# A four-layer graph network on one core: node rows lifted so that their mean carries the first norm's factor, and the first two node products joined

## The reference

```python
def _layernorm(x, axis=-1, eps=1e-05):
    m = jnp.mean(x, axis=axis, keepdims=True)
    v = jnp.var(x, axis=axis, keepdims=True)
    return (x - m) / jnp.sqrt(v + eps)
...
x = _layernorm(x + _L0_gnn_ref(x, edge_attr3_10x16, edge_index, ...))      # x + softplus MLP of summed edge rows
x = _layernorm(x + _L1_gnn_ref(x, edge_weight, src, dst, ...))             # (x W_self' + b + neighbours) / 2
x = _layernorm(x + _L2_gnn_ref(x, L2_gnn_w_s, L2_gnn_w_n, src, dst))       # relu(x w_s + neighbours)
x = _layernorm(x + _L3_gnn_ref(x, edge_index, ...))                        # two Chebyshev convolutions, hidden 256
return x
```

## Time and profile before

| | |
|---|---|
| three runs, median | 3864.7 us (3862.36 to 3864.95) |
| profiled execution | 3860.39 us, its span 3858.3 us |
| TensorE matmul busy | 3164.6 us, 82% of the span |
| VectorE busy | 3084.4 us, 80% |
| ScalarE busy | 2641.6 us, 68% |
| GpSimd busy | 2567.9 us, 67% |
| mean granted TensorE clock | 0.934 of 2.4 GHz |

### The profile page before, as it was taken

One profiled execution on the slowest core, in us unless ns is written; L12 is line 12 of the kernel. 1 busy time (PEld: TensorE's weight loads), 2 busy tenths in 40 slices (PEclk: granted clock), 3 DMA queues, 4 the chain that ended last, 5 costly groups with the idle time before them and its releaser, 6 DMA issues.

```text
span 3858.3 us, 74550 instructions
## 1 busy us (share of the span) xinstructions
PE 3164.6 (82%) x20774; PEld 2512.0 (65%) x20774; DVE 3084.4 (80%) x12882; ACT 2641.6 (68%) x7801; POOL 2567.9 (67%) x2650
## 2 busy tenths in 40 slices
PE   5779967777999999899999899989998999776100
PEld 2356656665888888678788766667777999665100
DVE  8979979997999999799899855557777888899200
ACT  0047769997888888699778777767766666698200
POOL 6757768884777777766477566645553666576676
PEclk9989979998999999999999999999999999988555
DMA  1056636564222222355455466657776777454432
GB/s 26 1 155 188 186 96 215 212 213 151 77 75 78 78 74 78 115 157 159 130 174 180 141 211 216 215 173 269 265 263 211 234 221 227 145 175 139 136 97 79
DMA packets 326132, 601.52 MB, mean 156 GB/s; under 512 B 71215, under 2 KB 99688, under 8 KB 325723
## 3 DMA queue, kind: packets, MB, share of 16 engines
q1 hardware_dynamic: 249434, 469.25, 36.3%
q0 software_dynamic: 76288, 127.51, 12.2%
HBM read 314.08 MB, written 283.99 MB: 155 GB/s over the span
## 4 chain that ended last, share of the span: by engine, by line
PE 47%; DVE 17%; POOL 15%; issue 9%; DMA 7%; ACT 4%; POOLq 1%; SPq 0%; DVEq 0%; ACTq 0%
PE ps L1670 7%; PE ps L1581 7%; PE ps L1528 6%; PE ps L1648 6%; PE ps L1727 4%; POOL rows L610 4%; POOL node_put L598 3%; POOL xin L610 3%; PE ps L1762 3%; DMA xin<-last_out 2%; POOL looked L676 2%; PE ps L1743 2%; PE ps L1742 2%; DMA out_dram<-xin,out_row 2%; DVE bn L949 2%
## 5 line engine op out<-in xcount | busy, mean ns | idle before, releaser
L610 POOL DMA_INDIRECT rows<-state,rows_of_src x588 | 556.9, 947 | 289.2 <-issue 153.9
L610 POOL DMA_INDIRECT rows<-lap,rows_of_lap x392 | 371.8, 949 | 266.2 <-PE ps L1687 123.3
L676 POOL DMA_INDIRECT looked<-node_table,look_idx x392 | 372.8, 951 | 111.1 <-issue 103.5
L646 POOL TENSOR_TENSOR y<-xin,c0h 128x512 f32<-128x512 f32 x245 | 313.7, 1280 | 174.7 <-DVE bn L949 83.0
L1134 DVE TENSOR_TENSOR_SCAN agg<-same,agg,ps 128x512 f32<-128x512 uint8 x288 | 366.0, 1271 | 56.2 <-PE ps L1687 50.9
L1670 PE MATMUL ps<-V,hT 128*128 128x128 f32 x3136 | 401.3, 282 | 3.6 <-ACT hT L1362 3.6
L1648 PE MATMUL ps<-yTc,G02c 128*128 128x512 f32 x784 | 382.1, 607 | 19.2 <-DVE y L1041 15.0
L949 DVE BATCH_NORM_STATS2 bn<-y 128x6 f32<-128x128 f32 x1764 | 374.4, 274 | 24.2 <-POOL y L646 24.1
L1670 PEld LDWEIGHTS ps<-V,hT 128*128 128x128 f32 x3136 | 375.6, 196 | 16.6 <-ACT hT L1362 4.4
L1528 PEld LDWEIGHTS ps<-ident,y 128*128 128x128 f32 x1960 | 236.8, 144 | 192.4 <-issue 168.0
L1528 PE MATMUL ps<-ident,y 128*128 128x128 f32 x1960 | 280.3, 278 | 77.3 <-POOL y L646 42.9
(11 more groups left out here) (286 smaller groups left out, 8892.5 us busy)
## 6 DMA issues: line engine op xcount, KB each, us to landing
state_h<-hb SPq DMA_DIRECT2D x98, 512.0 KB, 5.8
xin<-in_x_dram SPq DMA_DIRECT2D x196, 256.0 KB
out_dram<-outb SPq DMA_DIRECT2D x196, 256.0 KB
xe<-state SPq DMA_DIRECT2D x196, 256.0 KB
state<-outb SPq DMA_DIRECT2D x98, 256.0 KB
state<-oe SPq DMA_DIRECT2D x98, 256.0 KB
h_pre<-hb SPq DMA_DIRECT2D x49, 512.0 KB, 3.3
rows<-in_edge_attr_10x_dram SPq DMA_DIRECT2D x48, 320.0 KB, 3.3
```

What stands on the lines that cost most here:

```text
L610: gp.indirect_dma_start(out=dest[:, at, k, 0:width], out_offset=None, in_=table_, in_offset=bass.IndirectOffsetOnAxis(ap=index[:, c:c + 1] ...
L646: gp.tensor_tensor(y0[:, g.b], xin[:, g.r if p == "nodes" else g.b], all4(c0h[:, :]), ALU.add)\
L676: gp.indirect_dma_start(out=looked[:, c, 2 * j:2 * j + 2], out_offset=None, in_=node_table, in_offset=bass.IndirectOffsetOnAxis(ap=look_id ...
```

## The change

The first norm's factor is no longer taken out of the first product. VectorE adds to each y0 row the number sd - mean ("lift"), so that the row's mean becomes its standard deviation sd; the product's weights are centred except for a part that picks up the mean, so y1 comes out of the product scaled by sd with the offset b1 included, and the later norm takes the scale out again. A new weight matrix W12 of 256 columns holds that matrix and, beside it, its product with ws_sb; one product of 256 columns a row group gives both sd*y1 and sd*y1*w_s. y1 is not turned any more, and its copy of the turn, the reciprocal rs0 and the four y1 instructions of VectorE go, in "nodes" alone (src0 keeps them). ScalarE writes the relu of the second half to the y1 buffer and squares the first half out of PSUM; VectorE adds the first half to that relu for u2. The variance's eps is scaled by sd squared, which takes one more small VectorE instruction.

Order: in the alone stage the y0 turn moves to part 0 of its own turn on TensorE and on ScalarE, ahead of the x3 turn, and the joined product stands in part 1 behind the hidden product. In the shared stage the joined product of block g-1 opens part 0, into banks 5 and 6, which the hidden product of part 1 uses too; relu and squares follow the x3 copy in part 0 on ScalarE, the final activations move from part 0 to part 1 there, the store on SyncE from part 1 to part 2, and GpSimd makes y0 one block ahead in part 0, where it was two blocks ahead in part 1.

```diff
@@ weights, first stage @@
+                v.scalar_tensor_tensor(W12[:, 0:P], b1c[:, :], 1.0 / P, bank(6)[:, 0, :], ALU.mult, ALU.add)
...
+                v.tensor_copy(bcol, bank(7)[:, 2, :]).then_inc(vstep, 1)
+
+            def weights_twice():
+                dve.wait_ge(tstep, T_TWICE)
+                v.tensor_copy(W12[:, P:HID], bank(7)[:, 3, :])
...
@@ SyncE @@
-                if part == 1 and g4.inside(BLOCKS):
+                if part == (1 if q < PARTS * ALONE else 2) and g4.inside(BLOCKS):
...
@@ GpSimd @@
-                if part == (2 if alone else 1) and g.less(-2).inside(BLOCKS):
-                    if alone and g.less(2).inside(BLOCKS):
+                if not alone and part == 0 and g.c >= ALONE and g.less(-1).inside(BLOCKS):
+                    make_y0("nodes", g.less(-1))
+                if alone and part == 2 and g.less(-2).inside(BLOCKS):
+                    if g.less(2).inside(BLOCKS):
...
@@ VectorE, part 0 @@
-                    if g.inside(n):
-                        sd0.wait(dve, p, g)
-                        v.reciprocal(rs[:, 0, g.b, :], sd[:, 0, g.b, :]).then_inc(rs0.sem, 1)
+                    if shared and g.inside(n) and g.c >= ALONE:
+                        lift_rows(g)
...
                     if g1.inside(n):
-                        p2_made.wait(dve, p, g1)
-                        y1_made.wait(dve, p, g1)
-                        v.scalar_tensor_tensor(u2[:, g1.b], bank(4), 0.0, y1[:, g1.b], ALU.max, ALU.add)\
+                        relu_kept.wait(dve, p, g1)
+                        squared.wait(dve, p, g1)
+                        v.tensor_tensor(u2[:, g1.b], both(g1)[:, :, 0:P], y1[:, g1.b], ALU.add)\
                             .then_inc(u2_made.sem, 1)
-                    if g.inside(n):
-                        rs0.wait(dve, p, g)
-                        p1_made.wait(dve, p, g)
-                        y1_turned.wait(dve, p, g, back=2)
-                        squared.wait(dve, p, g, back=2)
-                        for k in range(4):
-                            i = v.scalar_tensor_tensor(y1[:, g.b, k, :], bank(6 if shared else 3)[:, k, :], dev(0, g.b, k),
-                                                       b1c[:, :], ALU.mult, ALU.add)
-                        i.then_inc(y1_made.sem, 1)
...
@@ VectorE, part 1 @@
+                        v.scalar_tensor_tensor(negm[:, g1.b, :], mv[:, 0, g1.b, :, 1], EPS * EPS, mv[:, 1, g1.b, :, 1],
+                                               ALU.mult, ALU.add).then_inc(var_kept.sem, 1)
+                        var_kept.wait(dve, p, g1)
...
@@ VectorE, part 2, ahead of x3 @@
+                    if not shared and gn.inside(n):
+                        lift_rows(gn)
...
+            def lift_rows(g):
+                p = "nodes"
+                sd0.wait(dve, p, g)
+                v.tensor_tensor(lift[:, g.b, :], sd[:, 0, g.b, :], mv[:, 0, g.b, :, 0], ALU.subtract).then_inc(lift_made.sem, 1)
+                lift_made.wait(dve, p, g)
+                v.tensor_tensor(y0[:, g.b], y0[:, g.b], lift[:, g.b, :].unsqueeze(2).to_broadcast([P, 4, P]), ALU.add)\
+                    .then_inc(y0_lifted.sem, 1)
...
@@ ScalarE, part 0 @@
+                    if not shared and g.inside(n):
+                        keep(p, g, y0T_kept, y0_turned, [(p1_made, 1)], yTa[:, :, :], 0)
                     if g2.inside(n):
                         keep(p, g2, x3T_kept, x3_turned, [(h_made, 1)], yTc[:, :, :], 0 if shared else 2)
-                    if g4.inside(n):
+                    if shared and g1.inside(n) and g1.c >= ALONE - 1:
+                        relu_and_squares(g1)
+                    if not shared and g4.inside(n):
...
 @@ ScalarE, part 1, behind the two hidden activations @@
-                    if gn.inside(n):
-                        keep(p, gn, y0T_kept, y0_turned, [(p1_made, 1)], yTa[:, :, :], 0)
+                    if g.inside(n):
+                        if shared:
+                            keep(p, g, y0T_kept, y0_turned, [(p1_made, 1)], yTa[:, :, :], 0)
+                    if shared and g4.inside(n):
+                        off3_made.wait(act, p, g4)
+                        out_st.wait(act, p, g4, back=2)
+                        for k in range(4):
+                            i = a.activation(outb[:, g4.b, k, :], y3[:, g4.b, k, :], ACT.Identity,
+                                             bias=off3[:, g4.b, k:k + 1], scale=rs[:, 3, g4.b, k:k + 1])
+                        i.then_inc(final_made.sem, 1)
...
@@ ScalarE, part 2 @@
-                    if g.inside(n):
-                        keep(p, g, y1T_kept, y1_turned, [(p2_made, 1)], yTb[:, :, :], 0 if shared else 1)
-                        squares(p, g)
...
+                    if not shared and g.inside(n):
+                        relu_and_squares(g)
+
+            def relu_and_squares(g):
+                p = "nodes"
+                p1_made.wait(act, p, g)
+                u2_made.wait(act, p, g, back=2)
+                a.activation(y1[:, g.b], both(g)[:, :, P:HID], ACT.Relu).then_inc(relu_kept.sem, 1)
+                tv2.wait(act, p, g, back=2)
+                squared.wait(act, p, g, back=1)
+                for k in range(4):
+                    i = a.activation(unused[:, k, :], both(g)[:, k, 0:P], ACT.Square, accum_out=ssum[:, g.b, k:k + 1])
+                i.then_inc(squared.sem, 1)
...
@@ TensorE, part 0 @@
-                    if g1.inside(n):
-                        y1T_kept.wait(pe, p, g1)
-                        u2_made.wait(pe, p, g1, back=1)
-                        if shared and g3.inside(n):
-                            y3_made.wait(pe, p, g3)
-                        products(p2_made, g1, 4, yTb, ws_sb)
-                    if g.inside(n):
-                        y0T_kept.wait(pe, p, g)
+                    if shared and g1.inside(n) and g1.c >= ALONE - 1:
+                        both_products(g1, g3)
+                    if not shared and g.inside(n):
+                        y0_lifted.wait(pe, p, g)
+                        y0T_kept.wait(pe, p, g, back=1)
+                        turn4(p, g, y0_turned, y0[:, g.b], 0)
                     if g2.inside(n):
                         x3_made.wait(pe, p, g2)
                         x3T_kept.wait(pe, p, g2, back=1)
+                        if shared and g1.inside(n):
+                            y0T_kept.wait(pe, p, g1)
                         turn4(p, g2, x3_turned, x3[:, g2.b], 0 if shared else 2)
-                    if g.inside(n):
-                        if shared and g3.inside(n):
-                            hidden.wait(pe, p, g3)
-                        y1_made.wait(pe, p, g, back=1)
-                        products(p1_made, g, 6 if shared else 3, yTa, A1)
...
@@ TensorE, part 1 @@
                         hidden.wait(pe, p, g2, back=1)
+                        if shared and g1.inside(n):
+                            u2_made.wait(pe, p, g1)
+                            squared.wait(pe, p, g1)
                         for j in range(2):
-                            if shared and j == 1 and g.inside(n):
-                                y1_made.wait(pe, p, g)
                             t.matmul(ps[:, 5 + j, :], G02c[:, j * P:(j + 1) * P], yTc[:].rearrange("p k d -> p (k d)"),
                                      start=True, stop=True).then_inc(h_made.sem, 1)
...
+                    if not shared and g.inside(n):
+                        both_products(g, g3)
+                    if shared and g.inside(n):
+                        y0_lifted.wait(pe, p, g)
...
+                        turn4(p, g, y0_turned, y0[:, g.b], 0)
@@ TensorE, part 2 @@
-                    if g.inside(n):
-                        y1_made.wait(pe, p, g)
-                        y1T_kept.wait(pe, p, g, back=1)
...
-                        turn4(p, g, y1_turned, y1[:, g.b], 0 if shared else 1)
...
+            def both_products(g, g_hidden):
+                p = "nodes"
+                y0T_kept.wait(pe, p, g)
+                if g.c >= ALONE - 1 and g_hidden.inside(BLOCKS):
+                    hidden.wait(pe, p, g_hidden)
+                u2_made.wait(pe, p, g, back=1)
+                squared.wait(pe, p, g, back=1)
+                for k in range(4):
+                    i = t.matmul(both(g)[:, k, :], yTa[:, k, :], W12[:, :], start=True, stop=True)
+                i.then_inc(p1_made.sem, 1)
```

More of the change, by code:

```diff
@@ L192, in gnn_kernel @@
         b1_col, bs_col, bn_col, sp_col = (sb(n, [P, 1]) for n in ("b1_col", "bs_col", "bn_col", "sp_col"))
-        consts = sb("consts", [P, 4])
-        EPS4, EPS1, EPS2, HALF = (consts[:, n:n + 1] for n in range(4))
+        consts = sb("consts", [P, 5])
+        EPS4, EPS1, EPS2, HALF, EPS3 = (consts[:, n:n + 1] for n in range(5))
+        W12 = sb("W12", [P, HID])
+        lift = sb("lift", [P, 2, 4])
         y0, y1, u2, x3, x3b, outb = (sb(n, [P, 2, 4, P]) for n in ("y0", "y1", "u2", "x3", "x3b", "outb"))
@@ L228, in wide, with both @@
```

(8 more changed lines are left out.)

42 lines of the change are left out of this document (21 added, 21 removed).

## The result

The changed kernel takes 3927.0 us (median of 4 runs, 3919.2 to 3932.1), the kernel before 3864.6: a ratio of 1.016, 95% interval 1.0147 to 1.0172. The forecast of 3904 had the sign, and its range (3866 to 3930) holds the result; it took 40 us for what are 62. The profiled execution has a span of 3925.2 us, 66.9 more than before.

The account below looks back on a forecast made before the run. TensorE was taken as the bound in most stages, VectorE equally full in alone, GpSimd in L2 and LA. Terms 28 - 7 - 7 - 6 + 31 + 0 + 1 = +40 on 3860.4 gave 3900, or 3904 as median; range 3866 to 3930.

Parts of the forecast that it names:

- the sign: Whole kernel: the change was forecast to make it slower, by 40 us; slower was given 0.78.
- T2's mechanism: Edge pass T2: ScalarE's hidden-row copies come later and hold TensorE's last product, 1.91 us per node turn, +31 us.
- the forecast wait: Stage of node turns without pass work: TensorE's hidden product waits 0.90 us a turn for ScalarE's x3 copy.
- L1, T1, LH: Three edge passes bound by TensorE: dropping the middle turn saves 0.44 us per node turn; -6, -7 and -7 us.
- Alone: 91 node turns without pass work: TensorE's cycle grows from 6.98 to 7.30 us, VectorE's to 7.24; +28 us.
- the last product, put at 1.96: TensorE, node turns without pass work: the last product's share of the forecast 7.30 us cycle.
- LA at 0: Edge pass LA: GpSimd's gathers set the turn, so the change costs 0 us, ends -5 and +8 (together with L2).
- 5.3 us from part 0's start: Edge pass stages: time until u2 releases the hidden product's banks; in L1 TensorE arrives at 6.0, covering it by 0.7.
- The seams at 0: Stretches between two passes, three node parts without pass work: the prediction had no term for them.
- One of the two waits is hidden: Rival: only T2's wait or only that of node turns without pass work appears; 3873 to 3876 us; chance 0.24.
- The clock falls: Rival: TensorE's pauses in node turns without pass work lower its clock, some 30 us more, 3930; chance 0.10 with other stalls.
- TensorE's count decides: Rival: without pass work, y0 turn to hidden product takes under 1.46 us, not 1.78; 3831 to 3846 us; chance 0.14.

## Why the prediction came out as it did

The sign was right, and so was T2's mechanism. In the alone stage the forecast wait is there, but another queue sets the turn. That 3927 lies inside the range is in part luck: LA and the seams lost some 40 us that the sum has at nothing, and T2 and the alone stage lost less than their terms.

- **L1, T1, LH.** The y1 turn's 0.44 went once a node turn: 0.49 in T1 and LH, with 0.05 from a joined product of 1.73 in place of two of 0.89 (the term's lower end, 1.70 for a pass without a fixed part, does not follow from the earlier trace rows, by which half of 512 columns is 1.78). In L1 0.28 went, as every other node turn kept 18.1 to 18.3; the hidden product did not wait for u2 there, as worked out.
- **Alone.** Both engines' cycles were forecast longer and nearly equal, 7.30 and 7.24; the turn is 7.15. The wait for the x3 copy is there (0.69 of idle time), but it was the wrong one to count: the runs show VectorE deciding. The term mis-sized on TensorE is the last product, put at 1.96 from the earlier trace rows, which starts the next instruction after 1.78 when nothing holds that up. Over the 85 turns measured the stage lost 15 us, where 88 turns were put at 28.
- **T2.** Mechanism and place were right. By TensorE's starts in both traces, part 1 came 1.20 later (forecast 1.33) and part 0 0.82 (1.02), less 0.43 in part 2 (0.44): 1.59 a node turn, not 1.91. Half of the difference is the squares, 0.17 cheaper from PSUM for four. The Trainium skill, page "VectorE: DVE Perf Modes", section on the TRN2 errata, gives the fixed costs from which the prediction worked out just that estimate; the trace agrees (0.25 us a square against 1.17 / 4 = 0.29).
- **LA at 0.** The step that failed: "GpSimd's gathers set the turn" was taken from the earlier trace rows for L2 and carried over to LA. It holds in L2 (16.11, where VectorE is as full, 229 of 230 us). In LA it held in the old kernel, and it ended when the late final activations and the hidden product's wait for u2 came together: 2.07 us a node turn, with GpSimd waiting. The wait itself had been priced, 5.3 us from part 0's start, but weighed against L1's, T1's and LH's pass work alone.
- **The seams at 0.** Left out. There the same 5.3 us have no pass work to cover them: waits of 3.2 us for u2.
- **The rivals.** "One of the two waits is hidden" fell: both appear. "The clock falls" named a loss that came in another stage, and there beside two waits. The alone stage, with a pause in every turn, shows a granted clock of 0.99; LA shows 0.75. The Trainium skill, page "TensorE: Matmul & The Clock Gate", section on psum-queue depth-cycling, tells of a kernel whose clock swung between its two levels as TensorE paused briefly between groups of matmuls: the alone stage does not show that with 0.69 us in every turn, nor L2 (clock 1.00) with one wait of 1.6 us for u2 in each, while LA shows the lower level behind two waits over 2 us a node turn. "TensorE's count decides" fell in the alone stage: from y0 turn to hidden product it took 1.82, above the point of 1.46. (Half of that rival's gain of 34 us would be 3848, not 3846.)

## What to carry to other kernels

Cost an edit in every stage in which its code runs, the seams above all: a wait that pass work covers by 0.7 us in one stage stands bare where that work is missing. When two engines' cycles come out equal, find which decides by changing the order of one alone; the pause that can be seen need not be the one that counts. On an in-order queue put a step that nobody waits for into the time in which the queue waits anyway: here that alone was worth 49 us, more than the 18 us that the change gained in L1, T1 and LH.

## What the runs showed unexpectedly

- A late step and a wait, each nearly free alone (LA 15.83 with the first, 16.11 with the second, 16.41 in the old kernel), cost 2 us a turn together. Behind the wait the hidden product's four passes take up to 3.75 instead of 1.88 us at the lower clock level; with the wait alone they are as slow, and the turn is no longer for it.
- Putting an independent instruction between two of VectorE's that depend on each other saves 0.12 us a pair; two of them in 91 turns were worth 20 us.
- The same joined product made earlier cost 41 us, since at the head of part 0 it had been the cover for the pass's work on VectorE in L1 and on ScalarE in T1.
